# A two-layer decoder kernel: the weights of its second self-attention loaded in pieces of 128 and 256 KB, each at a step of its own

## The reference

```
def _L1_attn_ref(x, w_q, w_k, w_v, w_o):
    q = jnp.einsum('bsd,hqd->bhsq', x, w_q)
    k = jnp.einsum('bsd,hqd->bhsq', x, w_k)
    v = jnp.einsum('bsd,hvd->bhsv', x, w_v)
    scores = jnp.einsum('bhsq,bhtq->bhst', q, k)
    causal = jnp.triu(jnp.ones((s, s), dtype=bool), k=1)
    masked = jnp.where(causal, -jnp.inf, scores)
    weights = jax.nn.softmax(masked / jnp.sqrt(jnp.float32(dq)), axis=-1)
    out = jnp.einsum('bhst,bhtv->bhsv', weights, v)
    cat = out.transpose(0, 2, 1, 3).reshape(b, s, -1)
    return jnp.einsum('bsf,df->bsd', cat, w_o)
...
x = x + _L1_attn_ref(_layernorm(x, axis=-1), L1_attn_w_q, L1_attn_w_k, L1_attn_w_v, L1_attn_w_o)
```

## Time and profile before

| | |
|---|---|
| median of 3 runs | 3018.18 us (3016.68 to 3021.74) |
| the profiled execution's own time | 3010.78 us |
| its span | 3008.8 us |
| mean granted clock | 0.867 |
| PE busy | 2276.8 us (76%) |
| DVE busy | 2175.1 us (72%) |
| self-attention of layer 2 in batch 0 | about 322 to 646 us, a step some 40 us |

### The profile page before, as it was taken

One profiled execution on the slowest core, in us unless ns is written; L12 is line 12 of the kernel. 1 busy time (PEld: TensorE's weight loads), 2 busy tenths in 40 slices (PEclk: granted clock), 3 DMA queues, 4 the chain that ended last, 5 costly groups with the idle time before them and its releaser, 6 DMA issues.

```text
span 3008.8 us, 50636 instructions
## 1 busy us (share of the span) xinstructions
PE 2276.8 (76%) x17470; PEld 1830.6 (61%) x17470; DVE 2175.1 (72%) x4246; ACT 1060.2 (35%) x2004; POOL 585.9 (19%) x666
## 2 busy tenths in 40 slices
PE   3667788868776877886877687888677777888875
PEld 3556666657465756664755565666565566666663
DVE  6765788866866578885776667888586666788767
ACT  2312444422432244442242224444224223444324
POOL 2111222212101122221101112222120102222220
PEclk8778899989777889998877789999877878999988
DMA  6001689840001078983000119897100014899600
GB/s 234 1 15 40 137 160 171 154 86 1 1 15 56 15 149 161 170 152 63 1 1 15 56 37 167 166 164 144 31 1 15 1 55 85 161 169 166 113 1 14
DMA packets 658407, 251.39 MB, mean 84 GB/s; under 512 B 613082, under 2 KB 633946, under 8 KB 657370
## 3 DMA queue, kind: packets, MB, share of 16 engines
q1 hardware_dynamic: 653978, 243.79, 41.4%
q10 hardware_dynamic: 4160, 4.19, 0.4%
HBM read 52.87 MB, written 10.49 MB: 21 GB/s over the span
## 4 chain that ended last, share of the span: by engine, by line
issue 38%; PE 23%; DVE 18%; DMA 11%; ACT 5%; POOL 4%; DVEq 1%; ACTq 0%; SPq 0%; POOLq 0%
DMA l_ptb<-l_phb 6%; PE ps L233 5%; PE ps L235 5%; PE ps L234 4%; DMA l_pts<-l_phs 4%; DVE nmax L1385 3%; PE ps L1289 1%; DVE l_k L1440 1%; DVE l_q L1444 1%; DVE l_phb L1391 1%; DVE l_phs L1391 1%; ACT l_q L1351 1%; PE ps L1271 1%; ACT xn L1347 1%; POOL d_pn L990 1%
## 5 line engine op out<-in xcount | busy, mean ns | idle before, releaser
L1385 DVE TENSOR_REDUCE nmax<-ps 128x1 f32<-128x1024 f32 (+7 forms) x512 | 383.3, 750 | 23.0 <-PE ps L1273 20.9
L1494 POOL CAST l_phb<-l_pb 128x1024 f16<-128x1024 f32 (+3 forms) x256 | 241.4, 943 | 654.1 <-ACT l_pb L1336 337.8
L1336 ACT ACTIVATE l_pb<-ps,nmax 128x1024 f32<-128x1024 f32 (+3 forms) x256 | 244.7, 956 | 283.5 <-DVE nmax L1385 282.7
L1271 PE MATMUL ps<-l_k,l_q 128*128 128x512 f32 (+3 forms) x768 | 319.1, 416 | 24.3 <-ACT l_ps L1336 23.9
L1391 DVE TENSOR_TENSOR l_phb<-l_pb,l_phb 128x1024 f16<-128x1024 f32 (+3 forms) x256 | 288.2, 1126 | 15.5 <-POOL l_phb L1494 13.4
L1272 PE MATMUL ps<-l_k,l_q 128*128 128x512 f32 (+3 forms) x768 | 270.1, 363 | 0.0
L1289 PE MATMUL ps<-l_v,l_ptb 128*128 128x64 f16 x4992 | 197.8, 197 | 34.2 <-DMA l_ptb<-l_phb 34.1
L1289 PEld LDWEIGHTS ps<-l_v,l_ptb 128*128 128x128 f16 x4992 | 177.1, 101 | 67.4 <-DMA l_ptb<-l_phb 41.1
L233 PE MATMUL ps<-xTh,l_w 128*128 128x512 f32 x256 | 123.1, 481 | 83.9 <-DVE l_q L1444 50.5
L1494 POOL CAST l_phs<-l_ps 128x128 f16<-128x128 f32 (+3 forms) x256 | 124.2, 485 | 319.1 <-DMA l_pts<-l_phs 169.6
L1271 PEld LDWEIGHTS ps<-l_k,l_q 128*128 128x128 f32 x768 | 156.0, 203 | 44.2 <-ACT l_ps L1336 29.8
(11 more groups left out here) (361 smaller groups left out, 6279.4 us busy)
## 6 DMA issues: line engine op xcount, KB each, us to landing
l_k<-xn SPq DMA_DIRECT2D x128, 256.0 KB, 4.1
l_w<-l_wqk_s SPq DMA_DIRECT2D x32, 512.0 KB, 4.8
l_wv<-l_wv_s SPq DMA_DIRECT2D x16, 512.0 KB, 6.0
xin<-in_x SPq DMA_DIRECT2D x4, 1024.0 KB, 5.5
m_w<-in_m_w SPq DMA_DIRECT2D x8, 512.0 KB, 4.4
m_w<-in_m_w SPq DMA_DIRECT2D x4, 1024.0 KB, 9.2
l_wo<-in_l_wo SPq DMA_DIRECT2D x16, 256.0 KB, 4.5
l_ptb<-l_phb SPq DMA_TRANSPOSE x256, 4.1
```

The source lines that it names most:

```text
L1271: pe.matmul(s[:, c0:c1], q, L["l_k1"][:, h, c0:c1], start=True, stop=False)
L1336: s.activation(l_numer(k)[:, 0:n], l_banks(k)[:, 0:n], ACT.Exp, bias=nmax[:, k % 4:k % 4 + 1], accum_out=lsum[:, h, k % NT:k % NT + 1]).th ...
L1385: v.tensor_reduce(nmax[:, k % 4:k % 4 + 1], l_banks(k)[:, 0:n], AX.X, ALU.max, negate=True).then_inc(q_["max"], 1)
L1494: g.tensor_copy(l_parts(k)[:, 0:cols], l_numer(k)[:, 0:cols]).then_inc(q_["hi"], 1)
```

## The change

The load of one pair's `l_w` (512 KB, one DMA) becomes four DMAs of 128 KB: high and low part (l), w_q and w_k (m). They stand at k = 2, 5, 8 and 13. The load of `l_wv` (512 KB) becomes two of 256 KB, at k = 7 and 10 of even steps; the wait ahead of it moves from k = 2 to k = 7. The load of `l_wo` stays whole (256 KB) and moves from k = 2 to k = 9. PE waits for the sum of all pieces. The first loads of a batch, ahead of its blocks, are cut in the same way and stay together.

```diff
                 if kind == "K" and g == 0:
-                    pe.wait_ge(q_[f"w{n % 2}"], (b * NQ + n // 2 + 1) * 16)
+                    pe.wait_ge(q_[f"w{n % 2}"], (b * NQ + n // 2 + 1) * 64)
...
                 if g == 0:
-                    pe.wait_ge(q_["wv"], (b * NQ + n + 1) * 16)
+                    pe.wait_ge(q_["wv"], (b * NQ + n + 1) * 32)
...
-        def l_load_w(sp, b, j):
-            sp.dma_start(f32(L["l_w"][:, j % 2]).rearrange("p l m c e -> p l (m c e)"), a["l_wqk_s"][:, :, j, :]).then_inc(q_[f"w{j % 2}"], 16)
-
-        def l_load_wv(sp, b, q):
-            sp.dma_start(f32(L["l_wv"][:]).rearrange("p l c e -> p l (c e)"), a["l_wv_s"][:, :, q, :]).then_inc(q_["wv"], 16)
+        def l_load_w(sp, b, j, part):
+
+            l, m = part // 2, part % 2
+            sp.dma_start(f32(L["l_w"][:, j % 2, l, m]).rearrange("p c e -> p (c e)"),
+                         a["l_wqk_s"][:, l, j, m * DC * P:(m + 1) * DC * P]).then_inc(q_[f"w{j % 2}"], 16)
+
+        def l_load_wv(sp, b, q, l):
+            sp.dma_start(f32(L["l_wv"][:, l]).rearrange("p c e -> p (c e)"), a["l_wv_s"][:, l, q, :]).then_inc(q_["wv"], 16)
...
             for j in range(2):
-                l_load_w(sp, b, j)
-            l_load_wv(sp, b, 0)
+                for part in range(4):
+                    l_load_w(sp, b, j, part)
+            for l in range(2):
+                l_load_wv(sp, b, 0, l)
             l_load_wo(sp, b, 0)
...
-                if j + 2 < HP and k == 2:
-                    sp.wait_ge(*lower(b, ("Q", j + 1 - 1, 1)))
-                    l_load_w(sp, b, j + 2)
-                if j % 2 == 0 and j + 2 < HP and k == 2:
-                    sp.wait_ge(*lower(b, ("V", j // 2, 3)))
-                    l_load_wv(sp, b, j // 2 + 1)
-                if j % 2 == 1 and j >= 3 and k == 2:
+                if j + 2 < HP and k in (2, 5, 8, 13):
+                    if k == 2:
+                        sp.wait_ge(*lower(b, ("Q", j, 1)))
+                    l_load_w(sp, b, j + 2, (2, 5, 8, 13).index(k))
+                if j % 2 == 0 and j + 2 < HP and k in (7, 10):
+                    if k == 7:
+                        sp.wait_ge(*lower(b, ("V", j // 2, 3)))
+                    l_load_wv(sp, b, j // 2 + 1, (7, 10).index(k))
+                if j % 2 == 1 and j >= 3 and k == 9:
                     sp.wait_ge(*lower(b, ("O", j // 2 - 1, 3)))
                     l_load_wo(sp, b, j // 2)
```

## The result

The changed kernel takes 3148.14 us (3143.91 to 3149.14, 4 runs), against 3017.43 us for the kernel before in the same comparison: a ratio of 1.0432, 95% interval 1.0412 to 1.0452. It is 130 us slower. The forecast was 142 us. A later comparison gave 1.0467 (1.0436 to 1.0498).

The account below looks back on a forecast made before the run. The kernel was taken as a chain of hand-overs with little slack on PE, DVE and the DMA engines. Terms of 78 + 27 + 37 = 142 us on 3018 us gave 3160 us, range 3055 to 3235 us.

Parts of the forecast that it names:

- Term 1: At task K of block (j+1,0), PE waits for the fourth piece of l_w, 24 loads: 78 us (54 to 114).
- the example: End of step 3, batch 0: task K begins 0.64 us before the fourth piece could be issued behind flip (4,1).
- the signs: Expected in the profile: 24 PE waits for l_w, 2.5 to 4 us each; flip (j,15) issued 1.5 to 3 us later.
- Term 2: Half clock after PE's new waits at task K: 20 places at 1.3 us, 27 us (0 to 64).
- Term 3: More SP issues ahead of flip (j,15): 59 us, less 7 for pauses and 15 for the removed burst, 37 us.
- A: PE's wait for the fourth piece at task K stays hidden; only term 3 is left: 3055 us, chance 0.10.
- B: Load bursts caused PE's waits for flips, so the change is faster: 2948 us, or 2983 us with half; chance 0.06.
- C: Fourth piece takes 4.8 us like the whole load, each wait brings 6.8 us of half clock: 3233 us, chance 0.12.
- D: No change in the kernel's time: gains and costs balance within 0.2%, chance 0.02.

Follow-up runs that it names:

- The filled kernel before: Nine extra matmuls on resident data at the first task K of pairs 2 to 7, added to the kernel before: 3076.3 us, 1.0223.
- the fourth piece alone late: Changed kernel with all pieces and l_wo back at k = 2, only the fourth piece of l_w at k = 13: 3105.22 us, 1.0303 of before.

## Why the prediction was right

**What bounds the kernel.** Right: PE, ACT and DVE go through task K together and have no stock of work. The filled kernel before shows it, 67.7 us of work for 67 us of time.

**Term 1, the fourth piece: 78 us forecast, some 54 us measured.** The mechanism was right in place, count and sign: 24 waits, none without the late piece. The size failed at one step, "I take 3.3 us" for the landing. The piece of the example took 2.4 us, and all 24 took 2.3 to 2.9 us, so the low end that I had set aside held; with 2.3 us the same working gives 54 us. I had taken the row of a load twice the size, 3.3 us, and let the queue ahead make up for the difference; the queue did not delay the piece. The Trainium skill's fit ("DMA: Bandwidth & Descriptors", section "Anatomy of one DMA"), which I gave as an estimate of 2.3 us for a piece, agrees with the 2.4 us, although it is made for transfers issued by GpSimd. The other input was that PE is at task K ahead of the end of flip (j+1,1) in 17 of 24 places and that this stays. It nearly stayed with the fourth piece alone late (16), but not in the change (11). The waits were therefore 0.9 to 3.4 us and not the 2.5 to 4 us of the signs.

**Term 2, the clock: 27 us forecast, some 27 us measured** as what is left of 81 us beside 54 us of waiting, good to 10 us, and 30 us as PE's longer busy time in the passes. The agreement is partly luck: I had counted 20 stretches of 3.4 us, 68 us at half clock, while the late piece made it 92 us more in the passes (from 164 to 256 us) and the stretch of the example was 6.8 us. I had also tied the clock to the wait for the piece alone. With the fourth piece at k = 11 that wait is gone and PE is still busy 34 us longer in the passes than in the kernel before, so the later flips of term 3 bring half clock too, which the forecast had nowhere.

**Term 3, the issues among the flips: 37 us forecast, 14 + 23 = 37 us measured, good to some 15 us,** and 10 us more for cutting, which the forecast put at nothing because the pieces move the same bytes. Flip (j,15) is issued 18.5 us after flip (j,8) on average over the 24 steps, where it was 16.5 us; the 2.0 us lie in the 1.5 to 3 us of the signs. That the net number was met doesn't show its two parts, the 59 us of issues and the 15 us of relief. The relief was there in SP's list: flip (0,8) holds SP for 1.8 us in the change, 3.76 us before. What it gave in time no run parts from the price of an issue. Leaving the term out would have missed it all.

**Sum.** 54 + 27 + 48 = 129 us, with 142 us forecast: a term 24 us too large and a price of 10 us left out.

**Rivals.** A (the wait stays hidden) falls with the 24 waits. B (the bursts caused PE's waits for flips) falls with the fourth piece at k = 11: it lands in time, the bursts are gone, and the kernel is 62 us slower than before, its waits for flips 40 us longer. C (4.8 us of landing) is what the whole load at k = 13 comes near to, not the piece. D falls with the 130 us.

## What to carry to other kernels

A load may be moved as late as its first use minus its landing, measured on the instruction list of the issuing engine and not in steps of the loop: here the table of k put the last piece behind a transfer that belongs to the step that uses it, and one line of that table cost 2.7%. A burst that the trace shows to delay transfers gives nothing back until one finds who waits for those. Where several engines pass one task in lock step, a delay there counts in full, and idle time of PE can be paid a second time through its clock: here some 27 us on top of 54 us.

## What the runs showed of the hardware

A 128 KB load landed 2.4 us after its issue although flips stood ahead of it in SP's list, the one just before issued 1.9 us earlier; 24 such loads took 2.3 to 2.9 us, and the whole 512 KB load took 4.2 to 4.9 us in the same place. A late start of 2.4 us on average for PE cost 1.5 times its length (81 us for 54 us of waiting, with the intervals 71 to 91 us), and the same place filled with work cost one time its length (67 us for 67.7 us): the difference goes with the granted clock, in the passes 0.94 without the late piece and 0.91 with it. Of the wait beyond that, another 2.2 us each time, about its own length was paid (41 to 51 us for 42 to 52 us).
